# An LSTM with residual on one core: x of steps 6 and 7 loaded behind the weights, and the passes of the first pause cut at step 5

## The chip, the cores and the metric

The kernel runs on one core of a Trainium2 chip. The metric is the device time of one execution in microseconds. The kernel before takes 2532.24 us, the median of three runs (2531.81 to 2532.51).

## What is computed

`x` is 32 sequences of 512 steps of 512 features, `h0` is 32 x 512, the two weight matrices `Wx` and `Wh` are 512 x 2048, the bias has 2048 numbers, all in float32. For each step, with `c` starting at zero:

```
a = x[:, t] @ Wx + b + h @ Wh
i, f, o = sigmoid of the first three quarters of a;  g = tanh of the last
c = f * c + i * g
h = o * tanh(c)
out[:, t] = x[:, t] + h
```

The step for `h @ Wh` needs the `h` of the step before, so the 512 steps are one chain.

## The kernel before

**Tiling.** The four blocks of 128 features lie side by side on the 128 partitions (4 blocks x 32 sequences). Every float32 operand is split into two float16 parts, `hi` and `lo` (the rest), and a product is three passes: hi x hi, hi x lo, lo x hi. One "pass" here is one call of `plain_add` (L350) or `recur_add` (L341): four matmuls of 32 columns of weights and 512 moving columns, one for each block of 32 partitions, for one `k` of the four blocks of the contraction. `recur` (L458) is the 12 passes of `h @ Wh` of one step; they can begin when the transposed `h` (`hT_hi`) of the step before is there. TensorE (PE) fills the pause between two `recur` calls with the `x @ Wx` passes of later steps.

**Plain steps and the loop.** The first 12 steps (`PLAIN`) take `x @ Wx` as 12 plain passes each (`plain_passes`, L377); later pairs of steps use a scheme with seven products in place of eight (L473 to L505), whose operands are sums of blocks of `x` and of `Wx`. The blocks of `Wx` for it are formed in place by eight accumulating transfers of 512 KB in SBUF which the POOL queue issues during the first steps (L261 to L274): each waits for the one that forms its source, the first two for the last half of the weights.

**The passes of the first pauses.** Steps 0 to 4 get their x passes before the recurrence begins (`AHEAD` = 5). Of step 5, four passes (`BEFOREHAND`) lie inside `first_step` (L438). After each `recur` of a plain step, PE takes the passes `passes_done(t - 1)` to `passes_done(t)`, which is `min(BEFOREHAND + 9 * (step + 1), 84)`: 4 to 13 in step 0, that is eight for step 5 and the first one for step 6; then nine in each step up to step 7 and eight in step 8. The passes for step 6 wait for its bank to be filled with the bias (`seed_plain`, L565) and for its `xp_hi` (`cast_plain`, L577), both on ScalarE (ACT).

**How x comes in.** `x_ring` has four slots of eight steps (a chunk). On the SP queue are, in this order (L298 to L316): x of steps 0 to 3 (two of four blocks, the other two on the ACT queue), `Wx` block 0 in two halves, x of steps 4 to 7 (`load_second`, four transfers of 64 KB, L245), the other `Wx` blocks, `Wh`, the last block in two halves, and then the chunks 1 to 3, each of four transfers of 128 KB and each behind a wait on `x_loaded` for the chunk before (L311). `x_loaded` counts 64 for each chunk; x of steps 4 to 7 is the first 64. POOL waits for the last half of the weights and then issues its transfers.

**How x is turned.** ACT copies a group of four steps from the ring to `x_now` (`copy_x`, L573), VectorE (DVE) transposes it in two instructions of 128 x 256, one for the even and one for the odd steps (`transpose_x`, L717), ACT casts each step to float16 (`cast_plain`, L577) and DVE takes the rest (`rest_plain`, L731). Group 1 (steps 4 to 7) is copied at L689 and turned at L892 and L893, all before step 0. Step 6's cast and rest come in step 0 (L621 and L813), step 7's in step 1. In step 0, ACT also copies group 2 (steps 8 to 11):

```
                if s % GROUP == 0 and left >= CHUNK:
                    if s == 0:
                        act.wait_ge(x_loaded, (c + 2) * X_DMA)
                    act.wait_ge(x_blocks_ready, blocks_count(c * 2 + s // GROUP + 1, 6))
                    copy_x(c * 2 + s // GROUP + 2)
```

In step 0 these are a wait for `x_loaded` at 128 (chunk 1 has landed) and one for `x_blocks_ready` at 4 (group 1 has been transposed). In ACT's step 0 the order is: gates (L603 to L606), `tanh_c`, `seed_plain(6)`, `cast_plain(6)`, the copy of group 2, `negate` of one weight block (L648). On DVE it is: the cell update, `h_hi` and its transposes, `h_full`, `h_lo` and its transpose, the last two `split_h_lo` (L851), `rest_plain(6)`, `form_bias` (L845). Every engine executes its instructions in this written order.

Of the kernel before, what the change touches and what calls it, by code (L numbers as in the profile page):

```python
# [52 lines left out]
BIAS_AT = 0  # L53

UNROLLED = -(-PLAIN // CHUNK) * CHUNK

# [15 lines left out]

def passes_done(step):

    return min(BEFOREHAND + 9 * (step + 1), PASSES * (PLAIN - AHEAD))


def lstm_residual(nc, x, h0, w_x, w_h, bias, out):
# [20 lines left out]
    with ExitStack() as ctx:  # L99
# [64 lines left out]
        h0_last_ready = sem("h0_last_ready")  # L164
        h0T_last_ready = sem("h0T_last_ready")
        x_first_loaded = sem("x_first_loaded")
        x_loaded = sem("x_loaded")
        out_stored = sem("out_stored")
        w_negated = sem("w_negated")
# [75 lines left out]
        def load_second(engine, j):  # L245

            engine.dma_start(in_ring(j, 0, GROUP, GROUP), x_v[j][:, GROUP:CHUNK, :]).then_inc(x_loaded, 16)

        def half_columns(gates):
            return slice(gates * HALF * J, (gates + 1) * HALF * J)  # L250
# [26 lines left out]
        def _(sp):  # L277
# [22 lines left out]
            for n in range(2 * J):  # L300
                if n in HALVED:
                    for gates, done in enumerate((w_half_loaded[n], w_loaded[n])):
                        cols = half_columns(gates)
                        sp.dma_start(w_raw[:, n, cols], w_v[n][:, cols]).then_inc(done, 16)
                    if n == 0:
                        for j in range(J):
                            load_second(sp, j)
                else:
                    sp.dma_start(w_raw[:, n, :], w_v[n]).then_inc(w_loaded[n], 16)  # L309
            for c in range(1, SLOTS):  # L310
                sp.wait_ge(x_loaded, c * X_DMA)  # L311
                load_x(c, c * CHUNK)
# [16 lines left out]
        def _(pe):  # L329
# [177 lines left out]
            def step(t, s, left, c, plain_steps=0):  # L507
                q, p = c * (BODY // 2) + s // 2, s // 2 % 2
                if plain_steps <= 0:
                    recur(t, (odd if s % 2 else even)[p])  # L510
                elif t == 0:
                    first_step()
                elif t == 1:
                    second_step()
                else:
                    recur(t, plain_bank(t))
                if plain_steps > 0:
                    plain_passes(passes_done(t - 1), passes_done(t))
# [27 lines left out]
        def _(act):  # L546
# [26 lines left out]
            def copy_x(group):  # L573

                nc.scalar.activation(x_now[:, :], x_ring[:, ring_of(group)], ACT.Copy).then_inc(x_now_ready, 1)

            def cast_plain(t):  # L577
                act.wait_ge(x_blocks_ready, blocks_count(t // GROUP, 1 + t % 2))
# [15 lines left out]
            def step(t, s, left, c):  # L594
# [25 lines left out]
                if plain_steps > X_SLOTS:  # L620
# [17 lines left out]
                for piece, (n, k) in enumerate(NEGATED):  # L638
                    if plain_steps > 0 and NEGATE_AT[piece] == t:
                        negate(n, k)  # L640
                for piece, (n, k) in enumerate(FORMED):
                    if plain_steps > 0 and CAST_AT[piece] == t:
                        act.wait_ge(w_formed[n, k], 16)
# [33 lines left out]
            for k in range(J):  # L677
# [5 lines left out]
                if k == 0:  # L683
                    act.wait_ge(bias_spread, 1)
                    nc.scalar.activation(bias_scaled[:, :], plain_banks[1][:, :], ACT.Copy).then_inc(bias_ready, 1)
                    for t in range(1, GROUP):
                        cast_plain(t)
                    act.wait_ge(x_loaded, X_DMA)
                    copy_x(1)  # L689
# [20 lines left out]
        def _(dve):  # L710
# [5 lines left out]

            def transpose_x(group, g, odd):  # L717

                dve.wait_ge(x_now_ready, group + 1)
# [3 lines left out]
                nc.vector.transpose(dst, src[:, :, odd, :, :]).then_inc(x_blocks_ready, 1)  # L723

            def combine(group, g, to, a, b, op, after):
                blocks = x_blocks[:, g % 2, :, :, :]
# [51 lines left out]
            def step(t, s, left, c):  # L778
# [28 lines left out]
                else:  # L807
                    if left >= 2 and plain_steps <= 1:
                        fill_og_odd(q + 1, (r + 1) % 2)
                    if left >= 6 and plain_steps <= 5:  # L810
                        rest_early(q + 3, r + 3)
                if plain_steps > X_SLOTS:
                    rest_plain(t + X_SLOTS)  # L813
                if left >= CHUNK:
# [69 lines left out]
            for k in range(J):  # L884
# [4 lines left out]
                if k == 0:  # L889
                    for t in range(1, GROUP):  # L890
                        rest_plain(t)
                    transpose_x(1, 1, 0)  # L892
                    transpose_x(1, 1, 1)  # L893
# [36 lines left out]
```

## Time and profile before

| | us |
|---|---|
| median of three runs | 2532.24 |
| the profiled execution | 2531.83 |
| its span in the profile | 2530.0 |
| PE busy | 2517.9 (100%) |
| DVE busy | 1985.2 (78%) |
| ACT busy | 1247.7 (49%) |
| POOL busy | 7.3 |

A row of a timeline has the start in us from the span's start, the duration, the engine, the line, the operation with its output and inputs, and how many are merged; in brackets is the idle time before it and what ended it. The start-to-start distance of two rows, not the duration, is what an instruction takes of its engine, since they overlap. PE is the matmuls, PEld the weight loads; PEclk is the granted clock of TensorE, 1.00 being full. 1.8 us of the profiled execution's time lie outside its span.

### The profile page before, as it was taken

The page shows a single profiled execution, that of the slowest core. Times are in us where ns is not written, and L with a number is a line of the kernel's source. Part 1 is how long each engine was busy: PE and PEld are TensorE (multiplying, and loading weights), DVE is VectorE, ACT ScalarE, POOL GpSimd, SP SyncE. Part 2 cuts the span into 40 slices and gives each one's busy share as a digit, 9 for nine tenths or more (in the row PEclk, how much of TensorE's full clock was granted, in tenths as well). Part 3 has the DMA queues.
Part 4 walks back from the last instruction along what each step waited for, and adds up shares of the span by engine and source line. Part 5 has one row for each costly group of instructions (what it writes and reads, how often), then busy time and mean ns, then how long its engine had stood idle before and what let it go on. Part 6 is the DMA issues. An engine that isn't in the chain of part 4 may idle for free.

```text
span 2530.0 us, 156040 instructions
## 1 busy us (share of the span) xinstructions
PE 2517.9 (100%) x67311; PEld 1799.9 (71%) x67311; DVE 1985.2 (78%) x8608; ACT 1247.7 (49%) x5271; POOL 7.3 (0%) x12
## 2 busy tenths in 40 slices
PE   9999999999999999999999999999999999999998
PEld 4677777777777777777777777777777777777776
DVE  8877777777777777777777777777777777777776
ACT  7544444444444444444444444444444444444444
POOL 1000000000000000000000000000000000000000
PEclk9999999999999999999999999999999999999999
DMA  8110101101011011010110110101101011011000
GB/s 236 35 25 25 33 17 33 33 17 33 20 29 33 17 33 27 22 33 17 33 33 17 33 25 25 33 17 33 33 17 33 21 28 33 17 33 28 22 17 18
DMA packets 142167, 80.16 MB, mean 32 GB/s; under 512 B 8621, under 2 KB 139837, under 8 KB 141373
## 3 DMA queue, kind: packets, MB, share of 16 engines
q1 hardware_dynamic: 140548, 75.40, 11.3%
q0 software_dynamic: 1152, 4.19, 0.9%
q8 instruction: 18, 0.29, 0.0%
q10 hardware_dynamic: 440, 0.20, 0.0%
q14 instruction: 9, 0.07, 0.0%
HBM read 42.02 MB, written 33.55 MB: 30 GB/s over the span
## 4 chain that ended last, share of the span: by engine, by line
PE 97%; DVE 1%; DMA 1%; SPq 0%; ACT 0%; issue 0%; DVEq 0%
PE odd L337 26%; PE even L343 26%; PE odd L343 26%; PE even L337 13%; PE s1t_sum L337 6%; DMA w_raw<-in_L_cond_Wh_dram 1%; PE plain_even L343 0%; DVE xw_lo L851 0%; PE even L356 0%; DVE c_state L775 0%; DVE f_c L765 0%; DVE hT_hi L714 0%; DVE i_g L770 0%; PE plain_more L343 0%; PE plain_odd L343 0%; SPq L309 0%
## 5 line engine op out<-in xcount | busy, mean ns | idle before, releaser
L765 DVE TENSOR_TENSOR f_c<-i_f,c_state 128x64 f32<-128x64 f32 x1024 | 232.3, 227 | 443.5 <-ACT i_f L603 443.5
L603 ACT ACTIVATE i_f<-odd 128x128 f32<-128x128 f32 x504 | 145.4, 295 | 535.7 <-PE odd L343 535.7
L343 PE MATMUL even<-hw_hi,hT_hi 128*32 128x512 f16 x4060 | 394.9, 379 | 0.6 <-DVE hT_hi L714 0.6
L343 PE MATMUL even<-hw_lo,hT_hi 128*32 128x512 f16 x4060 | 394.9, 379 | 0.0
L343 PE MATMUL odd<-hw_hi,hT_hi 128*32 128x512 f16 x4032 | 392.1, 379 | 1.2 <-DVE hT_hi L714 1.2
L337 PE MATMUL odd<-xw_hi,xT_hi 128*32 128x256 f16 x8000 | 391.8, 273 | 1.2 <-ACT odd L548 1.2
L343 PE MATMUL odd<-hw_lo,hT_hi 128*32 128x512 f16 x4032 | 392.1, 379 | 0.0
L337 PE MATMUL odd<-xw_lo,xT_hi 128*32 128x256 f16 x8000 | 391.8, 273 | 0.0
L337 PE MATMUL odd<-xw_hi,xT_lo 128*32 128x256 f16 x8000 | 391.7, 273 | 0.0
L603 ACT ACTIVATE i_f<-even 128x128 f32<-128x128 f32 x508 | 146.5, 294 | 426.0 <-PE even L343 426.0
L613 ACT ACTIVATE tanh_c<-c_state 128x64 f32<-128x64 f32 x1024 | 279.2, 273 | 100.1 <-DVE c_state L775 41.5
L714 DVE STREAM_TRANSPOSE hT_hi<-h_hi 128x64 f16<-128x64 f16 (+1 forms) x1023 | 252.1, 246 | 35.1
L343 PE MATMUL even<-hw_hi,hT_lo 128*32 128x512 f16 x4060 | 263.4, 379 | 0.0
L343 PE MATMUL odd<-hw_hi,hT_lo 128*32 128x512 f16 x4032 | 261.2, 379 | 0.0
L337 PEld LDWEIGHTS odd<-xw_hi,xT_hi 128*32 128x32 f16 x8000 | 213.9, 97 | 59.6 <-ACT odd L548 1.7
L775 DVE TENSOR_TENSOR c_state<-i_g,f_c 128x64 f32<-128x64 f32 x1024 | 229.5, 224 | 17.5
L337 PE MATMUL even<-xw_lo,xT_hi 128*32 128x256 f16 x4000 | 239.2, 273 | 0.0
L770 DVE TENSOR_TENSOR i_g<-i_f,g_gate 128x64 f32<-128x64 f32 x1024 | 224.7, 219 | 0.1
L337 PEld LDWEIGHTS odd<-xw_hi,xT_lo 128*32 128x32 f16 x8000 | 214.0, 97 | 4.3
L337 PEld LDWEIGHTS odd<-xw_lo,xT_hi 128*32 128x32 f16 x8000 | 214.0, 97 | 4.3
L792 DVE TENSOR_TENSOR h_hi<-o_gate,tanh_c 128x64 f16<-128x64 f32 x1022 | 211.4, 207 | 0.0
L337 PE MATMUL even<-xw_hi,xT_lo 128*32 128x256 f16 x4000 | 195.9, 273 | 0.0
(145 smaller groups left out, 4089.5 us busy)
## 6 DMA issues: line engine op xcount, KB each, us to landing
x_ring<-in_x_dram SPq DMA_DIRECT2D x252, 128.0 KB, 2.8
out_dram<-x_ring SPq DMA_DIRECT2D x252, 128.0 KB
w_raw<-w_raw POOLq DMA_DIRECT2D x8, 512.0 KB, 6.3
w_raw<-in_L_cond_Wx_dram SPq DMA_DIRECT2D x3, 1024.0 KB, 9.8
w_raw<-in_L_cond_Wh_dram SPq DMA_DIRECT2D x3, 1024.0 KB, 15.8
w_raw<-in_L_cond_Wx_dram SPq DMA_DIRECT2D x2, 512.0 KB, 4.9
w_raw<-in_L_cond_Wh_dram SPq DMA_DIRECT2D x2, 512.0 KB, 20.2
x_ring<-in_x_dram SPq DMA_DIRECT2D x6, 64.0 KB, 4.8
```

The costliest lines, as they stand in the source:

```text
L337: mm = nc.tensor.matmul(bank[j * N:(j + 1) * N, cols], x_part[:, pair, n, k * N:(k + 1) * N], w_part[:, n, k, j, :], start=False, stop=Fal ...
L343: mm = nc.tensor.matmul(bank[j * N:(j + 1) * N, :], hT[:, k * N:(k + 1) * N], w[:, k, j, :], start=False, stop=False, skip_group_check=True)
L603: nc.scalar.activation(i_f_half, bank_half, ACT.Sigmoid, scale=UNSCALE).then_inc(if_ready[two], 1)
L613: nc.scalar.activation(half_of(tanh_c[:, :], two), half_of(c_state[:, :], two), ACT.Tanh).then_inc(tanh_c_ready[two], 1)
L714: nc.vector.transpose(to[:, :].rearrange("p (k e) -> p k e", k=J)[:, k, :], part[:, :].rearrange("p (e k) -> p k e", k=J)[:, k, :]).then_i ...
L765: nc.vector.tensor_tensor(half_of(f_c[:, :], two), half_of(i_f[:, P:2 * P], two), half_of(c_state[:, :], two), ALU.mult)
L770: nc.vector.tensor_tensor(half_of(i_g[:, :], two), half_of(i_f[:, 0:P], two), half_of(g_gate[:, :], two), ALU.mult).then_inc(i_g_ready[two ...
L775: nc.vector.tensor_tensor(half_of(c_state[:, :], two), half_of(i_g[:, :], two), half_of(f_c[:, :], two), ALU.add).then_inc(c_ready[two], 1)
L792: nc.vector.tensor_tensor(half_of(h_hi[:, :], two), half_of(o_gate[:, :], two), half_of(tanh_c[:, :], two), ALU.mult).then_inc(h_hi_ready[ ...
```

## The change

The four transfers of `load_second` become eight of 32 KB: four for steps 4 and 5 (pair 0) where the four were, counted on a new semaphore, and four for steps 6 and 7 (pair 1) behind all the weights, counted on `x_loaded`. Group 1 is copied and transposed pair by pair (`copy_pair`, `transpose_pair`), pair 0 where the group was, pair 1 in step 0: on ACT after `seed_plain(6)`, on DVE behind `split_h_lo`. `cast_plain(6)` of ACT's step 0 moves behind the copy of group 2 and `negate`. `form_bias` moves from step 0 to step 1. `passes_done` becomes `min(12 + 9 * step, 84)`: in step 0 the passes 4 to 12 (the eight left of step 5), then nine in each step up to step 8.

```
--- before.py
+++ after.py
@@ -50,7 +50,7 @@
 NEGATE_AT = (-1, -1, 0, 1)
 CAST_AT = (1, 2, 3, 4, 5, 6, 7, 8)
 REST_AT = ((2, 2), (3, 3), (4, 4), (5, 5), (6, 6), (7, 7), (8, 8), (9, 10))
-BIAS_AT = 0
+BIAS_AT = 1
 
 UNROLLED = -(-PLAIN // CHUNK) * CHUNK
 
@@ -72,7 +72,7 @@
 
 def passes_done(step):
 
-    return min(BEFOREHAND + 9 * (step + 1), PASSES * (PLAIN - AHEAD))
+    return min(PASSES + 9 * step, PASSES * (PLAIN - AHEAD))
 
 
 def lstm_residual(nc, x, h0, w_x, w_h, bias, out):
@@ -164,6 +164,8 @@
         h0_last_ready = sem("h0_last_ready")
         h0T_last_ready = sem("h0T_last_ready")
         x_first_loaded = sem("x_first_loaded")
+        x_second_loaded = sem("x_second_loaded")
+        x_pair_ready = sem("x_pair_ready")
         x_loaded = sem("x_loaded")
         out_stored = sem("out_stored")
         w_negated = sem("w_negated")
@@ -242,9 +244,10 @@
         def load_first(engine, j):
             engine.dma_start(in_ring(j, 0, 0, GROUP), x_v[j][:, 0:GROUP, :]).then_inc(x_first_loaded, 16)
 
-        def load_second(engine, j):
-
-            engine.dma_start(in_ring(j, 0, GROUP, GROUP), x_v[j][:, GROUP:CHUNK, :]).then_inc(x_loaded, 16)
+        def load_second(engine, j, pair, loaded):
+
+            first = GROUP + 2 * pair
+            engine.dma_start(in_ring(j, 0, first, 2), x_v[j][:, first:first + 2, :]).then_inc(loaded, 16)
 
         def half_columns(gates):
             return slice(gates * HALF * J, (gates + 1) * HALF * J)
@@ -304,9 +307,11 @@
                         sp.dma_start(w_raw[:, n, cols], w_v[n][:, cols]).then_inc(done, 16)
                     if n == 0:
                         for j in range(J):
-                            load_second(sp, j)
+                            load_second(sp, j, 0, x_second_loaded)
                 else:
                     sp.dma_start(w_raw[:, n, :], w_v[n]).then_inc(w_loaded[n], 16)
+            for j in range(J):
+                load_second(sp, j, 1, x_loaded)
             for c in range(1, SLOTS):
                 sp.wait_ge(x_loaded, c * X_DMA)
                 load_x(c, c * CHUNK)
@@ -515,7 +520,7 @@
                 else:
                     recur(t, plain_bank(t))
                 if plain_steps > 0:
-                    plain_passes(passes_done(t - 1), passes_done(t))
+                    plain_passes(passes_done(t - 1) if t else BEFOREHAND, passes_done(t))
                 if s % 2 == 0:
                     if left >= 3 and plain_steps <= 2:
                         middle(q + 1, 1 - p)
@@ -574,8 +579,18 @@
 
                 nc.scalar.activation(x_now[:, :], x_ring[:, ring_of(group)], ACT.Copy).then_inc(x_now_ready, 1)
 
+            def copy_pair(pair):
+
+                rows = slice(2 * pair * P, 2 * pair * P + 2 * P)
+                nc.scalar.activation(x_now[:, rows], x_ring[:, GROUP * P:2 * GROUP * P][:, rows],
+                                     ACT.Copy).then_inc(x_pair_ready, 1)
+
             def cast_plain(t):
-                act.wait_ge(x_blocks_ready, blocks_count(t // GROUP, 1 + t % 2))
+                if t // GROUP == 1:
+
+                    act.wait_ge(x_blocks_ready, blocks_count(1, t // 2 % 2 + 1))
+                else:
+                    act.wait_ge(x_blocks_ready, blocks_count(t // GROUP, 1 + t % 2))
                 first = (A11, A21)[t % 2]
                 nc.scalar.activation(xp_hi[:, t % X_SLOTS, :, :].rearrange("p (h k) e -> p h (k e)", h=2),
                                      x_blocks[:, t // GROUP % 2, t // 2 % 2, first:first + 5:4, :],
@@ -617,7 +632,10 @@
                     seed_plain(t + BANKS)
                 if s % 2 == 0 and left >= 3 and plain_steps <= 2:
                     take_s1t1(q + 1)
-                if plain_steps > X_SLOTS:
+                if plain_steps == PLAIN:
+                    act.wait_ge(x_loaded, X_DMA)
+                    copy_pair(1)
+                if X_SLOTS < plain_steps < PLAIN:
                     cast_plain(t + X_SLOTS)
                 if s % 2:
                     if left >= 4 and plain_steps <= 3:
@@ -638,6 +656,8 @@
                 for piece, (n, k) in enumerate(NEGATED):
                     if plain_steps > 0 and NEGATE_AT[piece] == t:
                         negate(n, k)
+                if plain_steps == PLAIN:
+                    cast_plain(t + X_SLOTS)
                 for piece, (n, k) in enumerate(FORMED):
                     if plain_steps > 0 and CAST_AT[piece] == t:
                         act.wait_ge(w_formed[n, k], 16)
@@ -685,8 +705,9 @@
                     nc.scalar.activation(bias_scaled[:, :], plain_banks[1][:, :], ACT.Copy).then_inc(bias_ready, 1)
                     for t in range(1, GROUP):
                         cast_plain(t)
-                    act.wait_ge(x_loaded, X_DMA)
-                    copy_x(1)
+                    act.wait_ge(x_blocks_ready, blocks_count(0, 2))
+                    act.wait_ge(x_second_loaded, X_DMA)
+                    copy_pair(0)
                     act.wait_ge(banks_open, 1)
                     act.wait_ge(bias_ready, 1)
                     seed_plain(AHEAD)
@@ -716,11 +737,19 @@
 
             def transpose_x(group, g, odd):
 
-                dve.wait_ge(x_now_ready, group + 1)
+
+                dve.wait_ge(x_now_ready, group + 1 if isinstance(group, int) and group == 0 else group)
                 src = x_now[:, :].rearrange("p (q s e k) -> p q s k e", q=2, s=2, k=J)
                 first = (A11, A21)[odd]
                 dst = x_blocks[:, g % 2, :, first:first + 5:4, :]
                 nc.vector.transpose(dst, src[:, :, odd, :, :]).then_inc(x_blocks_ready, 1)
+
+            def transpose_pair(pair):
+
+                dve.wait_ge(x_pair_ready, pair + 1)
+                src = x_now[:, 2 * pair * P:2 * pair * P + 2 * P].rearrange("p (s e k) -> p s k e", s=2, k=J)
+                dst = x_blocks[:, 1, pair, :, :].rearrange("p (h b) e -> p b h e", h=2)[:, A11:A21 + 1:A21, :, :]
+                nc.vector.transpose(dst, src).then_inc(x_blocks_ready, 1)
 
             def combine(group, g, to, a, b, op, after):
                 blocks = x_blocks[:, g % 2, :, :, :]
@@ -809,6 +838,8 @@
                         fill_og_odd(q + 1, (r + 1) % 2)
                     if left >= 6 and plain_steps <= 5:
                         rest_early(q + 3, r + 3)
+                if plain_steps == PLAIN:
+                    transpose_pair(1)
                 if plain_steps > X_SLOTS:
                     rest_plain(t + X_SLOTS)
                 if left >= CHUNK:
@@ -889,8 +920,7 @@
                 if k == 0:
                     for t in range(1, GROUP):
                         rest_plain(t)
-                    transpose_x(1, 1, 0)
-                    transpose_x(1, 1, 1)
+                    transpose_pair(0)
                     for t in range(GROUP, X_SLOTS):
                         rest_plain(t)
             transpose_h(h_hi_ready[0], h_hi, hT_hi, hT_hi_ready[0], 1)
```

## Rows read from the trace of the kernel before

**Rows 1.** TensorE's waits over the whole run: in total, times, longest, us.
```profile
PE even L356 <- ACT xp_hi L580: 1.2, 1, 1.2
```
**Rows 2.** The chain that ended last, up to 34 us, in order of time.
```profile
8.20 21.40 DMA w_raw<-in_L_cond_Wh_dram
...
29.62 1.15 ACT hw_hi L651 x2
...
33.24 0.40 PE even L356 x4
```
**Rows 3.** Timeline of TensorE around steps 0 to 2.
```profile
30.98 1.04 PE L356 MATMUL plain_more<-xw_hi,xp_lo 128*32 128x512 f16 x16
33.24 0.40 PE L356 MATMUL even<-xw_hi,xp_hi 128*32 128x512 f16 x4 [1.22 <-ACT xp_hi L580]
...
36.69 1.05 PE L356 MATMUL even<-xw_lo,xp_hi 128*32 128x512 f16 x16
37.55 0.62 PE L356 MATMUL even<-xw_hi,xp_lo 128*32 128x512 f16 x8
38.14 0.40 PE L343 MATMUL odd<-hw_hi,hT_hi 128*32 128x512 f16 x4
```
**Rows 4.** Timeline of ScalarE from step 0 to the gates of step 1.
```profile
32.28 0.58 ACT L566 ACTIVATE even<-bias_scaled 128x512 f32<-128x512 f32 x1
...
33.00 0.61 ACT L575 ACTIVATE x_now<-x_ring 128x512 f32<-128x512 f32 x1
33.52 1.04 ACT L648 ACTIVATE w_raw<-w_raw 128x1024 f32<-128x1024 f32 x1
36.28 0.29 ACT L603 ACTIVATE i_f<-even 128x128 f32<-128x128 f32 x1 [1.72 <-PE even L343]
```
**Rows 5.** Timeline of VectorE, step 0 and parts of step 1.
```profile
32.28 0.24 DVE L714 STREAM_TRANSPOSE hT_hi<-h_hi 128x64 f16<-128x64 f16 x1
...
33.68 1.25 DVE L851 SCALAR_TENSOR_TENSOR hw_lo<-w_raw,hw_hi 128x512 f16<-128x512 f32 x2
34.85 0.28 DVE L735 TENSOR_TENSOR xp_lo<-x_blocks,xp_hi 128x128 f16<-128x128 f32 x1
...
37.84 0.25 DVE L714 STREAM_TRANSPOSE hT_hi<-h_hi 128x64 f16<-128x64 f16 x1
...
39.42 0.72 DVE L723 STREAM_TRANSPOSE x_blocks<-x_now 128x256 f32<-128x256 f32 x1
41.29 0.23 DVE L765 TENSOR_TENSOR f_c<-i_f,c_state 128x64 f32<-128x64 f32 x1 [1.15 <-ACT i_f L603]
```
**Rows 6.** SP's issues for chunks 2, 3 and 4 (landing of the last), POOL's first two.
```profile
30.98 3.06 SPq L280 DMA_DIRECT2D x_ring<-in_x_dram  x4
...
41.44 3.25 SPq L280 DMA_DIRECT2D x_ring<-in_x_dram  x4
...
72.92 1.87 SPq L280 DMA_DIRECT2D x_ring<-in_x_dram  x4
...
DMA to landing us min/median/max: 2.7/2.9/3.0
...
29.89 1.90 POOL L274 DMA_DIRECT2D w_raw<-w_raw  x2 [29.44 <-DMA w_raw<-in_L_cond_Wh_dram]
```
**Rows 7.** DMA by queue (packets, MB, share of 16 engines): 28 to 28.5, 31.0 to 34.2, 38 to 39 us.
```profile
q1 hardware_dynamic: 135, 0.06, 92.8%
...
q0 software_dynamic: 124, 0.51, 95.4%
...
q1 hardware_dynamic: 517, 0.25, 105.9%
```
**Rows 8.** Weight loads of TensorE at the start of the run.
```profile
1.60 0.15 PEld L532 LDWEIGHTS plain_more<-zeros 128*128 128x128 f16 x1 [0.28 <-issue]
2.03 0.15 PEld L532 LDWEIGHTS even<-zeros 128*128 128x128 f16 x1 [0.28 <-issue]
...
5.53 0.32 PEld L392 LDWEIGHTS s1t_sum<-zeros 128*32 128x32 f16 x8 [0.24 <-issue]
```

More of the change, by code:

```diff
@@ L52 @@
 REST_AT = ((2, 2), (3, 3), (4, 4), (5, 5), (6, 6), (7, 7), (8, 8), (9, 10))
-BIAS_AT = 0
+BIAS_AT = 1
 UNROLLED = -(-PLAIN // CHUNK) * CHUNK
@@ L73, in passes_done @@
 def passes_done(step):
-    return min(BEFOREHAND + 9 * (step + 1), PASSES * (PLAIN - AHEAD))
+    return min(PASSES + 9 * step, PASSES * (PLAIN - AHEAD))
 def lstm_residual(nc, x, h0, w_x, w_h, bias, out):
@@ L166, in lstm_residual @@
         x_first_loaded = sem("x_first_loaded")
+        x_second_loaded = sem("x_second_loaded")
+        x_pair_ready = sem("x_pair_ready")
         x_loaded = sem("x_loaded")
@@ L243, in load_first, with load_second @@
             engine.dma_start(in_ring(j, 0, 0, GROUP), x_v[j][:, 0:GROUP, :]).then_inc(x_first_loaded, 16)
-        def load_second(engine, j):
-            engine.dma_start(in_ring(j, 0, GROUP, GROUP), x_v[j][:, GROUP:CHUNK, :]).then_inc(x_loaded, 16)
+        def load_second(engine, j, pair, loaded):
+            first = GROUP + 2 * pair
+            engine.dma_start(in_ring(j, 0, first, 2), x_v[j][:, first:first + 2, :]).then_inc(loaded, 16)
         def half_columns(gates):
@@ L306, in _ @@
                         for j in range(J):
-                            load_second(sp, j)
+                            load_second(sp, j, 0, x_second_loaded)
                 else:
                     sp.dma_start(w_raw[:, n, :], w_v[n]).then_inc(w_loaded[n], 16)
+            for j in range(J):
+                load_second(sp, j, 1, x_loaded)
             for c in range(1, SLOTS):
@@ L575, in copy_x, with copy_pair @@
                 nc.scalar.activation(x_now[:, :], x_ring[:, ring_of(group)], ACT.Copy).then_inc(x_now_ready, 1)
+            def copy_pair(pair):
+                rows = slice(2 * pair * P, 2 * pair * P + 2 * P)
+                nc.scalar.activation(x_now[:, rows], x_ring[:, GROUP * P:2 * GROUP * P][:, rows],
+                                     ACT.Copy).then_inc(x_pair_ready, 1)
             def cast_plain(t):
-                act.wait_ge(x_blocks_ready, blocks_count(t // GROUP, 1 + t % 2))
+                if t // GROUP == 1:
+                    act.wait_ge(x_blocks_ready, blocks_count(1, t // 2 % 2 + 1))
+                else:
+                    act.wait_ge(x_blocks_ready, blocks_count(t // GROUP, 1 + t % 2))
                 first = (A11, A21)[t % 2]
@@ L619, in step @@
                     take_s1t1(q + 1)
-                if plain_steps > X_SLOTS:
+                if plain_steps == PLAIN:
+                    act.wait_ge(x_loaded, X_DMA)
+                    copy_pair(1)
+                if X_SLOTS < plain_steps < PLAIN:
                     cast_plain(t + X_SLOTS)
@@ L640, in step @@
                         negate(n, k)
+                if plain_steps == PLAIN:
+                    cast_plain(t + X_SLOTS)
                 for piece, (n, k) in enumerate(FORMED):
@@ L687, in _ @@
                         cast_plain(t)
-                    act.wait_ge(x_loaded, X_DMA)
-                    copy_x(1)
+                    act.wait_ge(x_blocks_ready, blocks_count(0, 2))
+                    act.wait_ge(x_second_loaded, X_DMA)
+                    copy_pair(0)
                     act.wait_ge(banks_open, 1)
@@ L717, in transpose_x @@
             def transpose_x(group, g, odd):
-                dve.wait_ge(x_now_ready, group + 1)
+                dve.wait_ge(x_now_ready, group + 1 if isinstance(group, int) and group == 0 else group)
                 src = x_now[:, :].rearrange("p (q s e k) -> p q s k e", q=2, s=2, k=J)
@@ L723, in transpose_x, with transpose_pair @@
                 nc.vector.transpose(dst, src[:, :, odd, :, :]).then_inc(x_blocks_ready, 1)
+            def transpose_pair(pair):
+                dve.wait_ge(x_pair_ready, pair + 1)
+                src = x_now[:, 2 * pair * P:2 * pair * P + 2 * P].rearrange("p (s e k) -> p s k e", s=2, k=J)
+                dst = x_blocks[:, 1, pair, :, :].rearrange("p (h b) e -> p b h e", h=2)[:, A11:A21 + 1:A21, :, :]
+                nc.vector.transpose(dst, src).then_inc(x_blocks_ready, 1)
             def combine(group, g, to, a, b, op, after):
@@ L811, in step @@
                         rest_early(q + 3, r + 3)
+                if plain_steps == PLAIN:
+                    transpose_pair(1)
                 if plain_steps > X_SLOTS:
@@ L891, in _ @@
                         rest_plain(t)
-                    transpose_x(1, 1, 0)
-                    transpose_x(1, 1, 1)
+                    transpose_pair(0)
                     for t in range(GROUP, X_SLOTS):
```

2 lines of the change are left out of this document (1 added, 1 removed).

## The prediction

> **What bounds the kernel now.** The busy table comes first: PE is busy for 2517.9 of 2530.0 us, so from some 80 us on the time is PE's work, which the change doesn't touch. What can move is the start, and whatever the start gains or loses stands in full at the end, since the 512 steps are one chain. PE's waits come next: the whole run has one wait that the change names, 1.2 us on ACT's `xp_hi` [rows 1]. The chain of waits shows how step 0 comes about: the last half of `Wh` on the DMA until 29.60, ACT's last two weight casts, the gates, and then the wait for the first pass of step 6 [rows 2]. PE's timeline shows that pass start at 33.24 after 1.22 us of idle; in steps 1 and 2 the passes between two `recur` calls nearly fill the pause, and `recur` of step 2 starts at 38.14 [rows 3]. That 38.14 is the mark against which I measure: from there a step takes what the loop of PE, gates, cell and transpose takes, and a shift goes through.
>
> **The passes of the first pause.** Four passes take 37.55 - 36.69 = 0.86 us, 0.215 each [rows 3]. In step 0 the pass for step 6 goes; PE's eight others end before 32.1 (30.98 + 1.04) [rows 3], and `hT_hi` is there at 32.28 + 0.24 = 32.52 [rows 5]. So `recur` of step 1 begins near 32.6 instead of 33.45, 0.9 us earlier, and its next wait, on the last `split_h_lo` (ends 34.93 [rows 5]), is met just as PE arrives there (11 passes after 32.6: 34.96). Its gates could be ready at 35.3 instead of 36.2. The pass isn't saved but moved: it goes into step 8, whose pause has one pass less before and, by the pattern of the pauses, room for it: 0.
>
> **The weights' lead.** 128 KB of x in packets of 512 bytes leave the ring ahead of `Wx` block 1, 256 packets, 16 on each of 16 engines. One such packet takes an engine 16 x 1.0 x 1.059 / 517 = 33 ns at best and 16 x 0.5 x 0.928 / 135 = 55 ns just ahead of the end of the weights [rows 7]; 16 of them are 0.5 to 0.9 us. The last half of `Wh` thus lands at 28.7 to 29.1 instead of 29.60. ACT, which waited 0.4 us for it, can gain about that much in step 0, no more, since PE's own gates are ready near 30.3 without any wait: -0.35. By the Trainium skill ("DMA: Bandwidth & Descriptors", specifications) packets of 512 bytes already run at line rate, 435 GB/s, which would make the lead 0.3 us; the rows above say more, and neither figure enters what follows.
>
> **What comes behind.** The four issues of pair 1 take the place in SP's order that chunk 1 had, so they are in the ring in time. They land about when the last weights landed before, 29.2 to 29.6: the same packets lie ahead of them. But SP now waits for `x_loaded` at 64, which is pair 1, before it issues chunk 1. Before, that wait was met at once and chunk 1 ran in the shadow of the weights, landed by 30.98 (SP goes on to chunk 2 there [rows 6]). Now chunk 1 is issued at about 29.5, and next to POOL's accumulating transfers, which are issued 0.3 us after the last weights: at 29.0 to 29.4 instead of 29.89 [rows 6]. Chunk 2 of before was in just this place: issued from 30.98, landed when SP goes on at 41.44, 10.5 us later, while a chunk alone takes 1.87 us of issue and 2.9 to land [rows 6]; from 31.0 to 34.2 the engines move nothing but one POOL transfer, 124 packets at 95% of all engines [rows 7]. The wait for chunk 1 is thus bounded by 29.5 + 1.5 + 2.9 = 33.9 (alone) and 41.4 (chunk 2's time unshifted). I take 40.0: POOL starts 0.5 to 0.9 us earlier than before and SP follows closer behind, so chunk 2's 41.4 less 1.4.
>
> **Who waits for it.** In step 0 ACT waits for `x_loaded` at 128, that is chunk 1, before `copy_x(2)`; before, it copied at 33.00 [rows 4]. The second wait of that copy, all of group 1 transposed, now stands behind DVE's `transpose_pair(1)`, which follows `split_h_lo`: 34.85 - 0.35 + about 0.65 (128 x 256 costs 0.72 in [rows 5]) = 35.1. Behind the copy are `negate`, then `cast_plain(6)`, then the gates of step 1. Start to start: copy 0.52, `negate` 1.04 less the overlap, 0.95, cast 0.2 [rows 4], so the gates of step 1 begin 1.67 us after the copy begins. With the copy at 40.05 they begin at 41.7 instead of 36.28 [rows 4]. `copy_pair(1)` itself stands in time that ACT now spends waiting: 0. DVE stands in `rest_plain(6)` meanwhile and is needed only after the gates: 0. `form_bias`, 0.42 us or less, goes to step 1 where DVE has 1.15 us idle [rows 5]: 0. Chunks 2 and 3 land later too, by up to 10 us, but the first that wants chunk 2 is step 8, past 66 us: 0.
>
> **PE in the meantime.** `recur` of step 1 is over near 35.0. The nine passes that follow start with step 6, which needs the cast: 40.05 + 1.47 + 0.3 = 41.8. Nine passes are 1.94, so `recur` of step 2 begins at 43.8 at full clock (`hT_hi` of step 1 is there at 41.7 + 1.8, by 36.28 to 38.09 before [rows 4, 5]): **+5.7 us** against 38.14. The copy's start less 34.35 is that shift for any landing.
>
> PE has then idled for nearly 7 us; the longest gap that the trace of before shows is 1.2 us [rows 1], and its granted clock is 1.00 throughout, so no row shows what such a gap does. The nearest rows are those of the start, after PE had done nothing: weight loads 0.43 apart (1.60, 2.03), 512 columns at 1.2 GHz, and spaced for full clock from 5.53 on [rows 8], 4.3 us after the first matmul at 1.20. Taken over: 4.3 us of work at half speed, 2.15 lost; from the other side, nothing if the clock holds, and at most some 3.3 if it stays low half as long again. I take 2.2, since the gap is more like the idle start than like 1.2 us. The Trainium skill ("TensorE: Matmul & The Clock Gate", the HAM clock gate) says that an array left idle goes back to the half clock and has to be kept busy to leave it; by that rule the 2.2 stands, without it the sum is +5.7.
>
> **Sum.** +5.7 (ACT held in step 0 by chunk 1) + 2.2 (half clock) = +7.9 us on the profiled execution's 2531.83, that is 2539.7. The median of the runs stands 0.4 above that execution, so I give 2540.1. The 0.9 and 0.35 us that the change wins are inside: they end in a wait.
>
> **The rivals.** A measurement of this kernel tells about 0.2%, 5.06 us, from no change.
> (a) *Chunk 1 late, clock holds.* For it: matmuls of one core only, never below 1.00 in the profile. Against: the start [rows 8]. +5.7, 2537.9, and 3.5 to 7 over the landings. Chance 0.14.
> (b) *Chunk 1 early.* SP's loads get to the engines ahead of POOL's: pair 1 lands only some 0.5 us behind the last weights and SP issues faster. Then DVE's transpose at 35.1 ends the wait, gates of step 1 begin at 36.8, PE's passes end at 38.9: +0.8, 2533.0; with one POOL transfer in between (3 us [rows 7]) the copy is at 36 to 38, +1.7 to +3.7, 2534 to 2536. Chance 0.18, against it that before no x packet moved while the first POOL transfer did [rows 7].
> (c) *Faster, as the pause alone would have it.* ACT isn't held at all, `recur` of step 1 and what follows come 0.9 + 0.35 earlier: 2531.0. That is decided by the copy's start: only at 33.4 or earlier (gates at 35.05 less 1.67) does it leave step 1 alone, and DVE's transpose behind `split_h_lo` already stands at 35.1. Chance 0.03.
> (d) *The pause gets no shorter*, because PE meets `split_h_lo` anyway: changes (c) alone, by 0.9; for the others it is free. Counted in them.
> The forecast itself, late chunk and slow clock: 0.62; 0.03 is for what I don't see.
>
> **How the numbers follow.** The forecast's case runs from +5.5 (landing 38, 1.7 lost) to +10.4 (41.4 and 3.3): 2537.7 to 2542.6. To leave no more than 2 in 10 outside, the range goes down over (a) and the upper part of (b), to 2534.0, and up to 2543.0. Slower by over 0.2% (over 2537.3): the forecast, half of (a) and a little of the rest, 0.70. Within 0.2%: the other half of (a), (b), (c): 0.28. Faster by over 0.2%: 0.02, no mechanism that I found gives it.
>
> **What would show it.** In the profile after: chunk 1's four issues (L280's place) at 29 to 30 instead of from 9.86, the next four at about 40; ACT's copy of group 2 with an idle of 5 to 7 us ended by an x load (not by DVE's transpose: that would be (b)); gates of step 1 near 41.7; PE idle from 35 to 42, then passes 0.43 us apart for some 4 us (0.215: (a)); and all later steps as long as before. PE's 1.22 us wait on `xp_hi` ahead of step 1's `recur` gone and `recur` starting at 32.3 to 32.6 would show the change doing what it says. I am wrong if chunk 1 has landed by 35, or if a later step is shorter than before.

## The result, and the profile after

The changed kernel takes 2538.61 us (median of 13 runs, 2537.03 to 2539.50); the kernel before, on the same chips, 2532.05 us. The ratio is 1.0024 with a 95% interval of 1.0017 to 1.0032: 6.6 us slower. The profiled execution took 2538.74 us, 6.91 more than that of before, and its span, 2536.9 us, is 6.9 us longer. Here and in the experiments a few executions took hundreds of us or more longer (one of the kernel before 11721 us); the ratios leave them out, the medians count them.

The waits of TensorE (PE) come first, as [rows 1] did: in total, times, longest, us.

```profile
PE even L361 <- ACT xp_hi L595: 5.9, 1, 5.9
PE odd L348 <- DVE hT_hi L735: 1.3, 1, 1.3
PE odd L342 <- ACT odd L553: 1.2, 1, 1.2
```

The wait that the change was to shorten is the same one, on ScalarE's (ACT's) cast of step 6, and has grown from 1.2 to 5.9 us. It is now the only large one. PE's timeline shows both halves of what happened, the rows that answer to [rows 3]:

```profile
32.15 0.40 PE L348 MATMUL even<-hw_hi,hT_hi 128*32 128x512 f16 x4 [0.40 <-DVE hT_hi L735]
...
34.52 0.40 PE L348 MATMUL even<-hw_lo,hT_hi 128*32 128x512 f16 x4
40.82 1.90 PE L361 MATMUL even<-xw_hi,xp_hi 128*32 128x512 f16 x16 [5.90 <-ACT xp_hi L595]
42.48 1.95 PE L361 MATMUL even<-xw_lo,xp_hi 128*32 128x512 f16 x16
44.19 0.67 PE L361 MATMUL even<-xw_hi,xp_lo 128*32 128x512 f16 x4
44.62 0.67 PE L348 MATMUL odd<-hw_hi,hT_hi 128*32 128x512 f16 x4
...
49.79 0.40 PE L348 MATMUL plain_even<-hw_hi,hT_hi 128*32 128x512 f16 x4
```

The recurrence of step 1 begins 1.3 us earlier than before (32.15 for 33.45). Then PE stands until 40.82, and its first passes come 0.43 us apart instead of 0.215. The recurrence of step 2 begins at 44.62 instead of 38.14 [rows 3], 6.5 us late, and that of step 3 at 49.79, 7.0 late (42.83 before). After it every step has the length that it had (4.69, then 4.88 us), so this is the whole loss. The cause stands in ACT's timeline, beside [rows 4]:

```profile
31.75 0.58 ACT L571 ACTIVATE even<-bias_scaled 128x512 f32<-128x512 f32 x1
32.27 0.40 ACT L585 ACTIVATE x_now<-x_ring 128x256 f32<-128x256 f32 x1
38.90 0.63 ACT L580 ACTIVATE x_now<-x_ring 128x512 f32<-128x512 f32 x1 [6.24 <-DMA x_ring<-in_x_dram]
39.44 1.04 ACT L668 ACTIVATE w_raw<-w_raw 128x1024 f32<-128x1024 f32 x1
40.39 0.29 ACT L595 ACTIVATE xp_hi<-x_blocks 128x128 f16<-128x128 f32 x1
40.59 0.26 ACT L618 ACTIVATE i_f<-even 128x128 f32<-128x128 f32 x1
```

Pair 1 is copied at once (32.27), then the copy of group 2 waits 6.24 us for chunk 1. Everything behind it on ACT is late: `negate`, the cast of step 6, and at 40.59 the gates of step 1, whose sums PE had ready at 34.9. VectorE (DVE) had transposed pair 1 by 35.0 (34.33 + 0.66) and isn't what the copy waited for:

```profile
34.33 0.66 DVE L752 STREAM_TRANSPOSE x_blocks<-x_now 128x256 f32<-128x256 f32 x1
```

The issues of SP and POOL, beside [rows 6]:

```profile
28.35 21.29 SPq L283 DMA_DIRECT2D x_ring<-in_x_dram  x12
...
27.99 1.91 POOL L277 DMA_DIRECT2D w_raw<-w_raw  x2 [27.54 <-ACT w_raw L668]
```

Chunk 1 is issued from 28.35 (before: from 9.86), 0.36 us behind POOL's first transfer, and lands at 38.9, after 10.5 us, as chunk 2 of before did. Last, the clock, by stretches of 4 us (busy PE, PEld, DVE, ACT, POOL, then the granted clock, DMA share, GB/s):

```profile
32.00:36.00 4.00, 2.77 (x48) 1.34 (x48) 2.88 (x9) 0.67 (x2) 0.86 (x1) 1.00 1.09 228
36.00:40.00 4.00, 0.00 (x0) 0.00 (x0) 0.00 (x0) 1.10 (x2) 0.83 (x1) 0.85 0.84 174
40.00:44.00 4.00, 3.18 (x32) 1.46 (x36) 3.12 (x16) 3.69 (x13) 0.89 (x2) 0.50 0.98 207
44.00:48.00 4.00, 4.00 (x65) 1.95 (x60) 0.67 (x2) 0.93 (x2) 0.86 (x1) 0.80 1.08 227
```

From 36 to 40 us PE does nothing; the granted clock falls within that stretch, stands at 0.50 (1.2 GHz) from 40 to 44, and is back within the next.

### The profile page after: what moved, and what is told of

It is laid out like the page before. It is cut to its first block, busy times and chain, and to the rows that moved or that the text cites. A ratio compares the mean times of both kernels' runs of the same rounds, so it can differ in the third digit from the quotient of the medians.

```text
span 2536.9 us, 156044 instructions
## 1 busy us (share of the span) xinstructions
PE 2519.9 (99%) x67311; PEld 1800.7 (71%) x67311; DVE 1986.0 (78%) x8608; ACT 1248.8 (49%) x5272; POOL 7.3 (0%) x12
## 4 chain that ended last, share of the span: by engine, by line
PE 97%; DVE 1%; DMA 1%; SPq 0%; ACT 0%; issue 0%; DVEq 0%
PE odd L342 26%; PE odd L348 26%; PE even L348 26%; PE even L342 13%; PE s1t_sum L342 6%; DMA x_ring<-in_x_dram 1%; PE even L361 0%; PE plain_even L348 0%; DVE xw_lo L882 0%; DVE c_state L804 0%; DVE f_c L794 0%; SPq L250 0%; DVE hT_hi L735 0%; DVE i_g L799 0%; PE plain_more L348 0%; SPq L312 0%
```

## The experiments

The theory: chunk 1, issued late and next to POOL's accumulating transfers, holds ACT in step 0 with the gates of step 1 behind the wait, and the idle time puts PE on its lower clock. The rivals: the new order of cast, copy and `negate` on ACT is itself the cost; the cut of the passes is; chunk 1 is slow whatever runs beside it.

**1. Chunk 1 not held.** Pair 1 gets a semaphore of its own, and the counts that include it are one chunk lower:

```
-                load_second(sp, j, 1, x_loaded)
+                load_second(sp, j, 1, x_pair_loaded)
             for c in range(1, SLOTS):
-                sp.wait_ge(x_loaded, c * X_DMA)
+                if c > 1:
+                    sp.wait_ge(x_loaded, (c - 1) * X_DMA)
```

> The changed kernel, but pair 1 counts on a semaphore of its own, so SP issues chunk 1 right behind it, without a wait, as the kernel before did. Theory (chunk 1, issued late and next to POOL's transfers, holds ScalarE in step 0): chunk 1 lands by about 31; the copy of group 2 is then held by VectorE's transpose of pair 1 alone and starts near 35.0 instead of 38.90; gates of step 1 at 36.7 (before 36.28, changed 40.59); TensorE idles about 2 us, its clock stays at 1.00; 2532.6 us, +0.8 over before (+0.3 to +1.5). Rival 1 (the new order on ScalarE, cast of step 6 behind copy and negate, is the cost): still +5 us or more. Rival 2 (the cut of the passes costs): the steps after the first show it, and it stays at +5 or more.

2533.54 us (10 runs) against 2532.70 for the kernel before beside it, ratio 1.0004 (0.9994 to 1.0014); the profiled execution took 2532.66 us, 0.8 over that of before, as expected. Its ACT timeline:

```profile
34.81 0.63 ACT L582 ACTIVATE x_now<-x_ring 128x512 f32<-128x512 f32 x1 [2.40 <-DVE x_blocks L754]
...
36.49 0.26 ACT L620 ACTIVATE i_f<-even 128x128 f32<-128x128 f32 x1
```

The copy now waits for DVE's transpose, and the clock stays at 1.00. Six of the 6.9 us are gone with one wait of SP's, while the order on ACT and the cut of the passes are still those of the change. Both those rivals fall as causes of the loss. What is left of them is small: the copy and `negate`, which the change put ahead of the cast of step 6, now wait for the transpose behind `split_h_lo`, and that uses up the lead of the pause. PE still waits 2.1 us, and the recurrence of step 2 begins at 38.67; run 7, where only the copy stands elsewhere, has it at 37.02. So the order on ACT costs some 1.5 us once chunk 1 is early (0.14 of the 1.65 is an earlier step 0).

**2. POOL after chunk 1.** SP as in the change, but POOL's first transfer waits until chunk 1 has landed:

```
             pool.wait_ge(w_loaded[2 * J - 1], 16)
+            pool.wait_ge(x_loaded, 2 * X_DMA)
```

> The changed kernel, with POOL's first accumulating transfer waiting until chunk 1 has landed. SP's order and waits are those of the change. Theory (it is the company of POOL's transfers that makes chunk 1 take 9 to 10 us): issued at 28.35 it lands at about 33, the copy of group 2 starts near 35.0 behind VectorE's transpose, gates of step 1 near 36.7; POOL's chain is 5 us later, so a cast of a formed block in step 1 or 2 may wait up to 2 us: +0.8 to +3 us over before. Rival (chunk 1 is slow by itself, 512-byte packets behind the weights): it still lands at 37 to 39 and the time stays at +6 or more.

One run: 2532.29 us, span 2530.5. SP issues chunk 1 at 27.67, and POOL, which waits for its landing, starts at 33.27. In the kernel before POOL started 0.29 us behind the landing that it waited for, so chunk 1 landed near 33.0: 5.3 us instead of 10.5. The copy starts at 34.80, right behind DVE's transpose (done at 34.72), and the gates at 36.48, as in run 1. No cast of a formed block waits, though POOL's chain runs 5 us late. So the company of POOL's transfers makes the landing late, not the loads' own length.

**3. TensorE kept busy.** The changed kernel with 24 passes of zeros in PE's idle time:

```
+                if plain_steps == PLAIN - 1:
+                    for _ in range(8):
+                        keep_going()
```

> The changed kernel, with 24 more passes of zeros into the scratch bank (5.2 us at full clock) between the recurrence of step 1 and the passes behind it, in TensorE's idle time. Theory (2.3 us of the loss are the half clock after the idle time): granted clock 1.00 throughout, the nine passes take 1.94 instead of 3.80 us, the recurrence of step 2 starts near 42.8 instead of 44.62; +4.6 us over before, 2536.4 (2536.0 to 2536.9). Rival (the clock costs nothing, the step waits for something else): unchanged at +6.5 to +7.

```profile
34.52 5.37 PE L397 MATMUL s1t_sum<-zeros 128*32 128x512 f16 x96
40.39 1.05 PE L361 MATMUL even<-xw_hi,xp_hi 128*32 128x512 f16 x16 [0.51 <-ACT xp_hi L598]
...
42.33 0.40 PE L348 MATMUL odd<-hw_hi,hT_hi 128*32 128x512 f16 x4
...
47.03 0.40 PE L348 MATMUL plain_even<-hw_hi,hT_hi 128*32 128x512 f16 x4
```

The clock stays at 1.00 and the nine passes take 1.94 us (40.39 to 42.33). Step 3 begins 2.76 us ahead of the changed kernel (47.03 for 49.79); 0.43 of that is a copy that started earlier (38.47 for 38.90), so the clock is worth 2.3 us. But the time was not what I expected: 2538.23 us, ratio 1.0022, only 0.4 below the changed kernel's, and the span 2536.5. PE's waits say where the rest went:

```profile
PE even L348 <- issue: 2.0, 1, 2.0
```

One stall of 2.0 us in which PE waited for nothing that the profile shows, in the last 30 us of the run, behind the step whose gates are at 2510. By its place, this is where the loop over the steps is left for the code behind it. The kernels before and after have no such stall.

**4. The cut of the passes alone,** on the kernel before:

```
-    return min(BEFOREHAND + 9 * (step + 1), PASSES * (PLAIN - AHEAD))
+    return min(PASSES + 9 * step, PASSES * (PLAIN - AHEAD))
```

> The kernel before with only the new cut of the passes (12 + 9 * step): loads, copies and the order on the other engines are untouched. Theory (the cut by itself wins what I worked out): the recurrence of step 1 starts at 32.6 instead of 33.45, idle 0.4 to 0.8 instead of 1.22, and the gain stays to the end: -0.9 us (-0.5 to -1.1), 2531.2; the pass moved to step 8 costs nothing. Rival (given back in step 8 or at the wait for the last split of Wh): 0 within 0.2 us.

2531.84 us against 2532.70, ratio 0.9998 (0.9988 to 1.0007); the medians differ by 0.9, which the interval does not part from nothing. The profiled spans are 2529.3 and 2530.0 us, a difference no larger than that between two executions of one kernel. The rows at the start say more: the gates of step 0 come 0.13 us later than before. Even so the recurrence of step 1 begins at 32.81, 0.6 us earlier, behind an idle of 0.59 instead of 1.22, and that of step 2 at 37.49 instead of 38.14. PE still waits 0.16 us before the recurrence of step 9, 0.37 in the kernel before: the ninth pass of step 8 fits. The cut does what it was worked out to do and is not the cause of the loss.

**5. The kernel before, chunk 1 held for the weights:**

```
+            sp.wait_ge(w_loaded[2 * J - 1], 16)
             for c in range(1, SLOTS):
```

> The kernel before with one wait more: SP waits for the last half of the weights before it issues chunk 1. Nothing else is changed. Theory (the late chunk 1 alone makes the loss): chunk 1 is issued near 29.7 beside POOL's transfers and lands near 39.5 to 40.5; ScalarE's copy of group 2 starts then, gates of step 1 behind copy and negate near 41.5 instead of 36.28; TensorE, whose nine passes don't wait here, idles from 38.2 to 43.3 and comes back at the half clock: +5.2 for the gates and up to 2.3 for the clock, 2538.5 (2537 to 2540). Rival (it takes the new order of cast, copy and negate too): +2 us or less.

A miss: 2532.10 us, ratio 0.9998 (0.9989 to 1.0007), no loss at all. The trace:

```profile
27.59 18.82 SPq L280 DMA_DIRECT2D x_ring<-in_x_dram  x12
...
27.87 1.90 POOL L274 DMA_DIRECT2D w_raw<-w_raw  x2 [27.42 <-DMA w_raw<-in_L_cond_Wh_dram]
...
34.99 0.63 ACT L576 ACTIVATE x_now<-x_ring 128x512 f32<-128x512 f32 x1 [2.22 <-DMA x_ring<-in_x_dram]
...
36.47 0.28 ACT L604 ACTIVATE i_f<-even 128x128 f32<-128x128 f32 x1
```

Chunk 1 was held, but SP got in 0.28 us ahead of POOL, and it landed in 7.4 us. The gates follow the copy by 1.48 us, as worked out, and 36.47 is just about where they were. Two things follow. Being issued late isn't enough: SP was ahead of POOL here and 0.36 us behind it in the change (what moved when is in the last section). And the last weights landed at 27.6 here, 2.0 us earlier than in the kernel before (29.60 [rows 2]), where chunk 1 was queued behind them. The same part of the kernel ran once more in run 9, and there POOL's row puts the landing at 28.35, 1.3 us earlier.

**6. The copy of group 2 in step 1, chunk 1 held as in the change:**

```
-                if s % GROUP == 0 and left >= CHUNK:
-                    if s == 0:
+                if (s % GROUP == 0 and left >= CHUNK and plain_steps != PLAIN) or plain_steps == PLAIN - 1:
+                    if s // GROUP == 0:
```

> The changed kernel, chunk 1 as late as there, but ScalarE's wait for it and the copy of group 2 stand in step 1 behind the cast of step 7 instead of in step 0. Theory (a late chunk costs by what stands behind its wait): chunk 1 still lands near 38.9, but the cast of step 6 and the gates of step 1 no longer wait for it; gates of step 1 near 35.0, those of step 2 behind copy, negate and the cast of a weight block near 41.3 instead of 40.97; TensorE's longest idle time 1 to 2 us, clock 1.00; 2532.2 us, +0.4 over before (-0.5 to +1). Rival (the late loads slow the start wherever the wait stands): +3 or more.

2532.10 us against 2532.51, ratio 0.9996 (0.9987 to 1.0006), span 2529.8. SP is 0.39 us behind POOL (27.87 and 27.48), and chunk 1 lands in 10.5 us:

```profile
35.42 0.27 ACT L618 ACTIVATE i_f<-even 128x128 f32<-128x128 f32 x1
...
38.41 0.63 ACT L580 ACTIVATE x_now<-x_ring 128x512 f32<-128x512 f32 x1 [0.61 <-DMA x_ring<-in_x_dram]
```

The load is as late as in the change (38.4 for 38.9), but the wait for it has nothing in front of it that the next recurrence needs, and 6.2 us of waiting shrink to 0.6. PE's longest wait for the cast is 0.55 us.

**7. Both mends together,** as a candidate for beating both kernels (edits of 1 and 6):

> Both mends together: pair 1 on a semaphore of its own, so chunk 1 isn't held, and the copy of group 2 in step 1. It is the candidate for beating both kernels. Theory: recurrence of step 1 at 31.9, its gates near 35.0 right behind it, the cast of step 6 when pair 1 is transposed at 34.8, recurrence of step 2 near 37.1 instead of 38.14; all of the lead of the pause and of the earlier weights stays: -1.0 to -1.4 us against before, 2531.0, and 0.3 to 0.6 below the passes alone. Rival (the transpose of pair 1 behind the last split of Wh holds the cast, and the gain is that of the passes alone): -0.9 or less.

2531.14 us (11 runs) against 2532.51, ratio 0.9994 (0.9985 to 1.0003); span 2528.8, 1.2 us under that of before, and 0.5 under that of the passes alone. The recurrence of step 2 begins at 37.02 (38.14 before), with 0.54 us of wait for the cast. By the profiled span it is the fastest of all; by the timed runs its lead of 1.4 us isn't told from none.

**8. As 3, with 18 passes of zeros:**

> As the run with TensorE kept busy in its idle time, with 18 passes of zeros in place of 24 (3.9 us). There step 3 was 2.8 us ahead of the changed kernel, but 2.0 us were lost at about 2510 us in one stall of TensorE's issue near the end, where the loop is left. Theory (the clock is worth 2.3 to 2.8 us; the stall at the end comes with the place of the code behind the loop, which moves with the 48 instructions fewer): clock 1.00 throughout, step 3 again 2.8 ahead, and if the stall is gone 2536.0. Rival (whatever the clock gives back at the start is lost at the end): the stall stays and the time is 2538.

2537.27 us, ratio 1.0018 (1.0009 to 1.0027), span 2535.6. The clock is 1.00, the gates of step 2 are 2.8 us ahead of the changed kernel's again (output gate at 45.67 for 48.47), and the stall near the end is there with 1.1 us in place of 2.0. So neither the theory (gone) nor the rival (as long as before) is right: with 24 matmuls fewer it is shorter, and still there.

**9. The kernel before, chunk 1 issued behind POOL's first transfer:**

```
+            sp.wait_ge(hw_hi_ready, J * GATES)
             for c in range(1, SLOTS):
```

> The kernel before with one wait more on SP: chunk 1 is issued only when the last cast of Wh is done, near 30.3, some 2.4 us after POOL's first transfer (held to the end of the weights, it was issued 0.3 us ahead of POOL and landed in 7.4 us). Theory (what counts is how many of POOL's transfers get in between): it lands near 40; the copy of group 2 starts then and the gates of step 1 1.47 us later, at 41.5 (+5.2); TensorE idles from 38 to 43 and its clock falls, +1.5 to +2.5: 2538.5 (2537 to 2540), the changed kernel's loss out of the kernel before with one wait. Rival (the loss needs the changed order on ScalarE and VectorE): +2 or less.

2539.76 us against 2531.85, ratio 1.0030 (1.0018 to 1.0042), 7.9 us slower: with this one wait the kernel before shows the whole loss.

```profile
31.18 21.11 SPq L280 DMA_DIRECT2D x_ring<-in_x_dram  x12
...
28.64 1.91 POOL L274 DMA_DIRECT2D w_raw<-w_raw  x2 [28.19 <-DMA w_raw<-in_L_cond_Wh_dram]
...
41.93 0.63 ACT L576 ACTIVATE x_now<-x_ring 128x512 f32<-128x512 f32 x1 [8.46 <-DMA x_ring<-in_x_dram]
...
45.23 0.62 PE L344 MATMUL odd<-hw_hi,hT_hi 128*32 128x512 f16 x4 [6.68 <-DVE hT_hi L715]
```

Issued 2.5 us behind POOL, it takes 10.75 us; the granted clock falls to 0.50 from 44 to 48 us here too.

**10. The changed kernel, POOL starting together with chunk 1:**

```
             pool.wait_ge(w_loaded[2 * J - 1], 16)
+            pool.wait_ge(x_loaded, X_DMA)
```

> The changed kernel, with POOL's first transfer waiting for pair 1 too, so that POOL and SP's chunk 1 start together at 28.35 instead of POOL 0.36 us ahead. Theory (the start order decides how many of POOL's transfers come between the four loads): chunk 1 lands in 7 to 8 us, near 35.7, instead of 10.5; copy of group 2 then, TensorE idle 2 to 3 us, clock 1.00: shift = copy's start less 34.35, +0.6 to +2 us, 2533.5. Rival (the two share the engines evenly whatever the order): lands near 38.9 and stays at +6 or more.

The profiled execution is as the theory had it: SP at 28.02, POOL at 28.55, the copy at 35.66 (7.6 us), PE's wait 2.8 us, clock 1.00, span 2531.5, 2533.31 us. But it is the fastest of ten: the others reach up to 2539.84, the median is 2537.31 and the ratio 1.0022 (1.0012 to 1.0032). Four of the other nine have a mean granted clock of 0.998, as runs of the changed kernel and of run 9 do and none of the kernel before beside them does. So with the two started this close, chunk 1 was probably late in most of them; that is argued, since no trace of such a run shows it.

**11. Unheld, with more code.** Run 1 with 72 matmuls of 32 columns in PE's idle time of step 1.

> The changed kernel with chunk 1 unheld, and 72 matmuls of 32 columns more (as many instructions as in the run with 18 passes of zeros) in the 2.1 us that TensorE idles in step 1: instructions, but hardly time. Theory (the stall near the loop's end comes with the number of instructions ahead of it): an issue stall of about 1.1 us shows up at about 2505 us, and the span is 1 us over the 2530.9 of the kernel without them. Rival (the stall belongs to the late start of the others): no stall, 2531.

```profile
PE s1t_sum L527 <- issue: 3.4, 1, 3.4
...
PE even L350 <- issue: 0.7, 1, 0.7
```

2536.79 us, span 2535.0. The small matmuls did cost time: PE stood for 3.4 us in the middle of them with nothing that the profile shows to wait for, and the clock fell (0.76 from 40 to 44 us). So the span says nothing on the question. The second line says something: the stall near the end is there, 0.7 us, in a kernel whose chunk 1 isn't late, and run 1, the same without the added code, has none.

## Why the prediction was right

The forecast, slower by some 8 us at 2540.1, in a range of 2534.0 to 2543.0, holds: 2538.61. Step by step:

| step | forecast | measured |
|---|---|---|
| recurrence of step 1 begins | 32.3 to 32.6 | 32.15 |
| chunk 1 issued | 29.5 | 28.35 |
| chunk 1 landed, copy of group 2 | 40.0, 40.05 | 38.90 |
| gates of step 1 behind the copy | 1.67 us | 1.69 us |
| PE's idle time | nearly 7 us | 5.9 us |
| shift without the clock (copy less 34.35) | +5.7 | +4.55 to +4.62 |
| half clock | +2.2 | +2.3 to +2.4 |
| sum, profiled execution | +7.9 | +6.9 |

*The mechanism* is shown from both sides: taken away by run 1 (SP's wait), run 2 (POOL beside it) and run 6 (what stands behind ACT's wait), and put into the kernel before by run 9 with one instruction. Rival (a), clock holds, falls by the clock row and runs 3 and 8. Rival (b), chunk 1 early, is what the profiled execution of run 10 shows, at +1.5 us, within the +0.8 to +3.7 given for it; between it and the forecast lies the start order, SP 0.28 and 0.53 us ahead of POOL in runs 5 and 10, and 0.36 to 0.39 behind in the changed kernel and runs 3, 6 and 8. The prediction's own times (POOL 29.0 to 29.4, SP about 29.5) had this order right. Rival (c), faster, was ruled out by the transpose at 35.1; it stands at 35.0, and run 7 shows what (c) is worth when ACT is freed: -1.2 us in the profiled span, for my -1.25. That this agrees is in part luck: the recurrence of step 1 came 1.7 us earlier there, and 0.5 us of it went into a wait for the cast.

*The term that was mis-sized* is the start of chunk 1 and POOL. "The last half of `Wh` thus lands at 28.7 to 29.1", and pair 1 "at 29.2 to 29.6: the same packets lie ahead of them". SP's issue at 28.35 shows pair 1 landed more than 0.8 us sooner. I had counted only what was taken away ahead of the last weights. In the change chunk 1 no longer queued behind them either, and that counts as well: the last weights landed at 29.60 in the kernel before, 0.29 us ahead of POOL's first row. Taken from that row, they landed at 28.3 to 28.6 in runs 1, 7 and 11 (128 KB less ahead of them, chunk 1 still behind), and at 27.6 and 28.35 in runs 5 and 9 (nothing less ahead, chunk 1 not behind). In the changed kernel, where both came together, they landed at 27.7, and in runs 3, 6 and 8, which have the same loads, at 27.2 to 27.35. So 128 KB ahead were worth 1.0 to 1.3 us (I had 0.5 to 0.9), 512 KB behind 1.3 and 2.0 us in the two traces that show it (I had 0), and both together 1.9 to 2.4. The duration of 10.5 us, taken over from chunk 2 of before, was right to 0.1 us. So the 1.15 us by which the copy came earlier than I gave are all in the start, 28.35 for 29.5.

Two small slips in the sum had no weight. By its own terms (1.47 + 0.3 + 1.94 behind the copy) the shift is the copy less 34.43, not 34.35; measured at full clock it is the copy less 34.28 (run 1: 34.81 and 38.67). And I had put the median 0.4 us above the profiled execution, from three runs of the kernel before; here it lies 0.1 below. That is 0.5 of the 1.5 us between 2540.1 and 2538.61; the other 1.0 is the sum.

*The clock.* The granted clock was at 0.50 over the stretch behind the idle time, 1.2 of its 2.4 GHz, and PE had stood for 5.9 us before (6.7 in run 9). After waits of 2.1 us (runs 1 and 2) and 2.8 us (run 10) it was at 1.00. By the Trainium skill ("TensorE: Matmul & The Clock Gate", the HAM clock gate) an idle array goes back to the half clock; the rows agree, and the price taken from the start's rows, 4.3 us of slow work [rows 8], fits the 4.8 us from 40.82 to about 45.6 here. On the packets of 512 bytes, where that skill ("DMA: Bandwidth & Descriptors", specifications) gives line rate and so, as an estimate, 0.3 us for the lead, the traces disagree: 1.0 to 1.3 us.

*The small gains* were there. Gates of step 0 began at 30.10 instead of 30.68, 0.6 us for my 0.35: PE's own sums were ready earlier too (its last matmuls on the weights begin at 29.42 for 29.69), which I had taken as fixed. None of it reached the end.

## What to carry to other kernels

When a load is moved behind another, look at the loads that wait for it in the issuing queue, and for each ask what will run beside it at its new time: here 128 KB moved cost the chunk behind it the shadow of the weights, and its 10 us came out in the wait of an engine that had nothing to do with the move. Put a wait for a load on an engine behind everything that the next step of the chain needs from that engine: the same late load cost 6 us in step 0 and, by the timed runs, nothing that can be told from zero one step on. And price a TensorE gap of several microseconds at more than its length; here it was 5.9 us and 2.3 for the slow work behind it, while gaps of 2.1 and 2.8 us cost their length alone.

## What the runs showed of the hardware

The four loads of chunk 1 took 5.3 us with no accumulating transfer beside them (run 2), 7.4 and 7.6 when issued 0.3 and 0.5 us ahead of POOL's first (runs 5, 10), and 10.4 to 10.75 when issued 0.36 to 2.5 us behind it (changed kernel, runs 3, 6, 8 and 9). The packets that the two queues moved in each us show why:

| from, us | 28 | 29 | 30 | 31 | 32 | 33 | 34 | 35 | 36 | 37 | 38 |
|---|---|---|---|---|---|---|---|---|---|---|---|
| changed kernel, loads | 0 | 159 | 116 | 34 | 47 | 437 | 25 | 55 | 193 | 10 | 12 |
| changed kernel, POOL | 0 | 4 | 43 | 42 | 41 | 34 | 47 | 44 | 50 | 52 | 51 |
| run 5, loads | 70 | 396 | 109 | 44 | 99 | 370 | 0 | 0 | 33 | 41 | 32 |
| run 5, POOL | 0 | 7 | 45 | 44 | 43 | 30 | 54 | 58 | 52 | 44 | 32 |

Chunk 1 is 1088 packets by these rows. While one of POOL's transfers moves, the loads get 10 to 116 packets in a us, against 455 alone (run 2, from 29); about three quarters of chunk 1 go before POOL's first transfer and in the gaps between two. In run 5 466 packets were through by 30 and the rest by 34, behind one transfer. In the changed kernel only 159 were through by 30, the gap at 33 and that at 36 were both needed, and the last 22 packets moved beside a third transfer. So a start 0.64 us later against POOL put one whole transfer more and part of another ahead of the landing, which came 3.1 us later. The start order is a matter of tenths of a us, which would also explain why the times of run 10 spread over 6.5 us; those of the changed kernel spread over 2.5, no more than those of the kernel before beside it (2.4).

Loads queued behind others on the same queue put off the completion of those ahead by 2.0 us in run 5 and 1.3 in run 9. By which path isn't shown.

PE stalled near the end of the run, with nothing that the profile shows to wait for: 2.0, 1.1 and 0.7 us in the three kernels with 96 and 72 matmuls more in step 1, none in the others. Each comes behind the step whose gates are at 2510 and is known from one profiled execution. The stall doesn't need a late chunk 1 (run 11). That it is the fetch of the code behind the loop is my reading of its place; it wasn't tried by itself and stays open, as does why 96 matmuls make it longer than 72.
